# Half of the next head's rows ahead of a head's attention product, in an eight-head graph attention kernel on one core

## The reference

```python
h = (x @ W).reshape(n, H, C)
alpha_s = jnp.einsum('nhc,hc->nh', h, a_s)
alpha_d = jnp.einsum('nhc,hc->nh', h, a_d)
e = jax.nn.leaky_relu(alpha_s[src] + alpha_d[dst], NEG_SLOPE)
m = jax.ops.segment_max(e, dst, num_segments=n)
e = jnp.exp(e - m[dst])
alpha = e / (segment_sum(e, dst)[dst] + EPS)
out = segment_sum(h[src] * alpha[:, :, None], dst)
...
h = gat_layer(x, W1, a_src1, a_dst1, b1, edge_index, concat=True)
h = jax.nn.elu(h)
out = gat_layer(h, W2, a_src2, a_dst2, b2, edge_index, concat=True)
x = _layernorm(x + out, axis=-1)
```

## Time and profile before

| | before |
|---|---|
| median of 3 runs | 640.83 us (640.81 to 641.07) |
| the profiled execution | 641.08 us |
| its span in the profile | 639.3 us |
| TensorE busy | 632.1 us (99%) |
| VectorE, ScalarE, GpSimd busy | 518.9, 337.8, 204.4 us |

### The profile page before, as it was taken

One profiled execution on the slowest core, in us unless ns is written; L12 is line 12 of the kernel. 1 busy time (PEld: TensorE's weight loads), 2 busy tenths in 40 slices (PEclk: granted clock), 3 DMA queues, 4 the chain that ended last, 5 costly groups with the idle time before them and its releaser, 6 DMA issues.

```text
span 639.3 us, 9306 instructions
## 1 busy us (share of the span) xinstructions
PE 632.1 (99%) x3426; PEld 542.7 (85%) x3426; DVE 518.9 (81%) x928; ACT 337.8 (53%) x570; POOL 204.4 (32%) x122
## 2 busy tenths in 40 slices
PE   9999999999999999999999999999999999999996
PEld 6766568989888889988898889988998899887885
DVE  8999997889989987475855685567898589889876
ACT  7899992546524754353545454463545444534382
POOL 1000000140743630357124822374136604551230
PEclk9999999999999999999999999999999999999999
DMA  8422402115154420234113330316025401800002
GB/s 313 166 75 75 154 20 99 50 54 194 51 148 140 158 74 1 60 91 148 50 51 91 97 110 25 95 45 183 26 90 159 123 26 51 293 28 1 1 2 99
DMA packets 22173, 59.36 MB, mean 93 GB/s; under 512 B 2544, under 2 KB 2800, under 8 KB 22128
## 3 DMA queue, kind: packets, MB, share of 16 engines
q1 hardware_dynamic: 21984, 58.69, 28.6%
q10 hardware_dynamic: 144, 0.07, 0.0%
HBM read 54.03 MB, written 4.72 MB: 92 GB/s over the span
## 4 chain that ended last, share of the span: by engine, by line
PE 82%; DVE 16%; issue 1%; DMA 0%; ACT 0%; DVEq 0%
PE O L1238 30%; PE R L1136 8%; PE R L1133 8%; PE R L1139 8%; PE R L1205 6%; PE R L1211 6%; PE R L1208 6%; DVE ohd L679 4%; DVE ohs L683 2%; PE O L1150 2%; DVE junk L717 2%; DVE junk L736 2%; PE R L1155 1%; DVE W1l L705 1%; PE O L1205 1%
## 5 line engine op out<-in xcount | busy, mean ns | idle before, releaser
L1066 POOL TENSOR_TENSOR W2l<-Wr,W2h 128x768 fp32r<-128x768 f32 x48 | 93.3, 1953 | 207.8 <-ACT W2h L411 207.8
L1070 POOL TENSOR_TENSOR Pl<-L,Ph 128x512 fp32r<-128x512 f32 x34 | 54.0, 1599 | 166.7 <-ACT Ph L460 166.4
L1133 PE MATMUL R<-W1h,xTh 128*128 128x384 f32 x312 | 105.8, 339 | 0.0
L1139 PE MATMUL R<-W1h,xTl 128*128 128x384 f32 x312 | 104.9, 336 | 0.0
L1136 PE MATMUL R<-W1l,xTh 128*128 128x384 f32 x312 | 104.8, 336 | 0.0
L717 DVE CUSTOM_DVE_ANT_0 junk<-h,abc 128x768 bf16<-128x768 f32 x64 | 62.6, 978 | 41.8 <-ACT h L423 37.4
L1238 PE MATMUL O<-W2h,gh 128*128 128x256 f32 (+1 forms) x384 | 78.6, 339 | 0.0
L1238 PE MATMUL O<-W2h,gl 128*128 128x256 f32 (+1 forms) x384 | 77.4, 336 | 0.0
L1238 PE MATMUL O<-W2l,gh 128*128 128x256 f32 (+1 forms) x384 | 77.3, 335 | 0.0
L423 ACT COPY h<-R 128x384 f32<-128x384 f32 x62 | 29.5, 477 | 73.0 <-PE R L1139 70.9
L1060 POOL TENSOR_TENSOR W1l<-Wr,W1h 128x768 fp32r<-128x768 f32 x30 | 55.4, 1868 | 37.5 <-ACT W1h L400 37.5
(11 more groups left out here) (186 smaller groups left out, 1171.5 us busy)
## 6 DMA issues: line engine op xcount, KB each, us to landing
Wr<-in_W SPq DMA_DIRECT2D x101, 384.0 KB, 3.3
abc<-in_as SPq DMA_DIRECT2D x9, 384.0 KB, 4.0
abc<-in_ad SPq DMA_DIRECT2D x9, 384.0 KB, 5.9
h_rows<-h SPq DMA_DIRECT2D x8, 384.0 KB, 2.4
hl<-h_rows SPq DMA_DIRECT2D x8, 384.0 KB, 5.9
xin<-in_xT SPq DMA_DIRECT2D x6, 256.0 KB, 6.1
xr<-in_x SPq DMA_DIRECT2D x1, 1536.0 KB, 7.5
out<-res SPq DMA_DIRECT2D x4, 384.0 KB, 2.3
```

Source lines behind the costliest of these rows:

```text
L1066: e.tensor_tensor(W2l[:, m % N2, :], Wr[:, n, :], W2h[:, m % N2, :].bitcast(f32), ALU.subtract).then_inc(s_w2l, 1)
L1070: e.tensor_tensor(Pl[:, t, d0:d1], L[:, t, d0:d1], Ph[:, t, d0:d1].bitcast(f32), ALU.subtract).then_inc(s_Pl, 1)
L1133: e.matmul(bank[:, 0:HALF], xTh[:, f, xs], hi[:, ws], start=f == 0, stop=False)
L1139: m = e.matmul(bank[:, 0:HALF], xTl[:, f, xs], hi[:, ws], start=False, stop=f == FT - 1)
```

## The change

On TensorE, from head 3 on, the first four halves of B of head h+1 (tiles 0 and 1) are multiplied between the fifth and the sixth step of C(h-1), before den and A of head h; the other four stand at the start of head h+1 as before. `targets` moves from behind the second step of C to behind the third (heads 3 to 6). RING follows. On the other engines the work is written in another order around this, and the six pairs of products with the last layer's vectors are placed anew: pairs 0, 1 before the scores of head 5, pairs 3, 4 before those of head 6, pair 2 in head 6 and pair 5 in head 7 behind a tile's row sums. No instruction of arithmetic is added or taken away.

```diff
-    V_OF = {H - 3: range(0, 3), H - 2: range(3, 6)}
+    V_ROWS, V_SCORES = {H - 2: (2,), H - 1: (5,)}, {H - 3: (0, 1), H - 2: (3, 4)}
...
-    for h in range(EARLY, H):
-        RING += [("B", h, n) for n in range(8)]
-        RING += [("as", h, 0), ("r2", h, 0), ("r1", h, 0), ("den", h, 0)] + [("A", h, c) for c in range(FT)]
+    for h in range(EARLY, H + 1):
+        RING += [("B", h, n) for n in range(4) if h < H]
+        RING += [("den", h - 1, 0)] + [("A", h - 1, c) for c in range(FT)]
+        if h < H:
+            RING += [("B", h, n) for n in range(4, 8)] + [("as", h, 0), ("r2", h, 0), ("r1", h, 0)]
...
# scalar_program, head h
+                    if h + 1 < H:
+                        high_w1(h + 1, 0)
+                        high_w1(h + 1, 1)
                     high_w2(h - 1, 4)
+                    scores(h, h, 0, NT, ring_bank("r2", h, 0), (gl_value(h - 1, FT - 1), (s_g, FT * h)), 3 * h + 2,
+                           lambda u, h=h: high_w1(h + 1, 1 + u) if h + 1 < H and 1 <= u <= 4 else None)
+                    if h + 1 < H:
+                        evict_B(h + 1, 0, 0)
+                    high_sums(h)
                     high_w2(h - 1, 5)
+                    if h + 1 < H:
+                        evict_B(h + 1, 0, 1)
+                        high_w2(h, 0)
+                        evict_B(h + 1, 1, 0)
+                        high_w2(h, 1)
+                        evict_B(h + 1, 1, 1)
+                        high_w2(h, 2)
...
# vector_program, head h
-                    for t in range(NT):
+                    for t in (2, 3):
...
                     maxima(h, 0, NT, ring_bank("as", h, 0))
+                    if h + 3 == H:
+                        wait_abc(H)
+                    for i, k in enumerate(V_SCORES.get(h, ())):
+                        products_W2(k, 0 if i else 8 * h + 8)
                     scores(h, h, 0, NT, ring_bank("r1", h, 0), 3 * h + 3)
                     sums_P(h)
...
+                if 2 <= h < H - 1:
+                    wait_abc(h + 1)
+                    for t in range(2):
+                        e.wait_ge(s_h32, 8 * (h + 1) + 2 * t + 2)
+                        sums_h(h + 1, t, h32[:, t, :], abc[:, abc_slot(h + 1)[0], :, :])
                 if h:
                     reciprocals(h)
...
# gpsimd_program, head h
                 if h >= EARLY:
-                    for k in range(FT):
-                        low_w2(h - 1, k)
+                    if h + 1 < H:
+                        low_w1(h + 1, 0)
+                        low_w1(h + 1, 1)
+                    low_w2(h - 1, 4)
+                    if h + 1 < H:
+                        for k in range(2, FT):
+                            low_w1(h + 1, k)
                 for t in range(NT):
                     low_P(h, t, 0, N)
-                if EARLY <= h < H - 1:
-                    for k in range(FT):
-                        low_w1(h + 1, k)
+                if h >= 2:
+                    low_w2(h - 1, 5)
+                    if h + 1 < H:
+                        for k in range(4):
+                            low_w2(h, k)
...
# tensor_program, head h
                 if h >= EARLY:
-                    for n in range(8):
+                    for n in range(4, 8):
                         half_B(h, n // 2, n % 2, take("B", h, n))
                 for c in range(2 if h == 1 else 0, FT):
+                    if c == FT - 1 and 2 <= h < H - 1:
+                        for n in range(4):
+                            half_B(h + 1, n // 2, n % 2, take("B", h + 1, n))
                     stage_C(h - 1, c, between=(lambda h=h: denominators(h)) if c == FT - 1 else None,
                             at=1 if h == H - 1 else 2)
-                    if c == (0 if h == 2 else 1) and h > 1:
+                    if c == (0 if h == 2 else 1 if h == H - 1 else 2) and h > 1:
                         targets(h, 0, NT, (None, None), 2 * h + 2)
```

More of the change, by code:

```diff
@@ L37, in gat_resnorm_kernel @@
     for h in range(EARLY, H):
-        LOADS += [("w2", h - 1, k) for k in range(FT)]
-        LOADS += [("w1", h + 1, k) for k in range(FT) if h + 1 < H]
-        LOADS += [("v", H - 1, k) for k in V_OF.get(h, ())]
+        LOADS += [("w2", h - 1, k) for k in range(4)] + [("v", H - 1, k) for k in V_ROWS.get(h, ())]
+        LOADS += [("w2", h - 1, 4)] + [("w1", h + 1, k) for k in range(2) if h + 1 < H]
+        LOADS += [("v", H - 1, k) for k in V_SCORES.get(h, ())]
+        LOADS += [("w1", h + 1, k) for k in range(2, FT) if h + 1 < H] + [("w2", h - 1, 5)]
     LOADS += [("w2", H - 1, k) for k in range(FT)]
@@ L51, in gat_resnorm_kernel @@
     RING += [("as", 2, 0), ("den", 1, 0)] + [("A", 1, c) for c in range(FT)]
-    RING += [("r2", 2, 0), ("r1", 2, 0), ("den", 2, 0)] + [("A", 2, c) for c in range(FT)]
-    for h in range(EARLY, H):
-        RING += [("B", h, n) for n in range(8)]
-        RING += [("as", h, 0), ("r2", h, 0), ("r1", h, 0), ("den", h, 0)] + [("A", h, c) for c in range(FT)]
+    RING += [("r2", 2, 0), ("r1", 2, 0)]
+    for h in range(EARLY, H + 1):
[3 more added lines that the diff above has]
+            RING += [("B", h, n) for n in range(4, 8)] + [("as", h, 0), ("r2", h, 0), ("r1", h, 0)]
     RING += [("al", H, 0), ("at", H, 0), ("as", H, 0), ("r2", H, 0), ("r1", H, 0), ("tail", 0, 0)]
@@ L335, in sync_program @@
             for h in range(EARLY, H):
+                if h + 2 < H:
+                    load_abc(h + 1)
+                for k in range(4):
+                    load_raw("w2", h - 1, k)
+                for k in V_ROWS.get(h, ()):
+                    load_raw("v", H - 1, k)
+                load_raw("w2", h - 1, 4)
                 if h + 1 < H:
[L337 to L339 removed]
+                    load_raw("w1", h + 1, 0)
+                    load_raw("w1", h + 1, 1)
+                if h + 3 == H:
+                    load_abc(H)
                 if h + 2 == H:
                     load_abc(H - 1)
+                for k in V_SCORES.get(h, ()):
+                    load_raw("v", H - 1, k)
                 if h + 1 < H:
[L343 removed]
+                    for k in range(2, FT):
                         load_raw("w1", h + 1, k)
[L345 to L346 removed]
+                load_raw("w2", h - 1, 5)
             for k in range(4):
@@ L565, in scalar_program @@
                     high_sums(2)
+                    evict_B(3, 0, 0)
                     high_h(2, 2)
                     high_h(2, 3)
+                    high_w2(1, 5)
+                    evict_B(3, 0, 1)
+                    high_w2(2, 0)
+                    evict_B(3, 1, 0)
+                    high_w2(2, 1)
+                    evict_B(3, 1, 1)
+                    high_w2(2, 2)
                 if 0 < h < EARLY:
@@ L603, in scalar_program @@
                 for c in range(FT):
+                    if c == FT - 1 and 2 <= h < H - 1:
+                        high_h(h + 1, 0)
                     exp_y(h, c)
+                    if c == FT - 1 and 2 <= h < H - 1:
+                        high_h(h + 1, 1)
                     if c:
                         high_g(h, c - 1)
+                    if c == FT - 1 and 2 <= h < H - 1:
+                        evict_B(h + 1, 2, 0)
                     if h == 0 and c < 2:
@@ L614, in scalar_program @@
                         high_w1(3, c - 2)
-                    if EARLY <= h < H - 1 and c < 2:
-                        high_w1(h + 1, 4 + c)
+                    if 2 <= h < H - 1 and c == 1:
+                        high_w2(h, 3)
                     if h == H - 1 and c == 0:
@@ L714, in sums_h @@
                         e.wait_ge(s_asd, n)
-                    if not i and h - 1 in V_OF and t in range(1, 4):
-                        e.wait_ge(s_v, 2 * V_OF[h - 1][t - 1] + 2)
+                    if not i and t == 0 and h - 1 in V_SCORES:
+                        e.wait_ge(s_v, 2 * V_SCORES[h - 1][-1] + 2)
+                    if not i and t == 3 and h in V_ROWS:
+                        e.wait_ge(s_v, 2 * V_ROWS[h][-1] + 2)
                     e.tensor_tensor_reduce(
@@ L730, in products_W2 @@
                 for i in range(2):
-                    if i:
-                        e.wait_ge(s_v, 2 * k + 1)
+                    if i or not ready:
+                        e.wait_ge(s_v, 2 * k + i)
                     else:
@@ L945, in vector_program @@
                         low_h(h, t)
[L946 to L949, removed]
+                        if t == 2:
+                            for k in V_ROWS.get(h, ()):
+                                products_W2(k, 8 * h + 6)
                     maxima(h, 0, NT, ring_bank("as", h, 0))
+                    if h + 3 == H:
+                        wait_abc(H)
+                    for i, k in enumerate(V_SCORES.get(h, ())):
+                        products_W2(k, 0 if i else 8 * h + 8)
                     scores(h, h, 0, NT, ring_bank("r1", h, 0), 3 * h + 3)
@@ L968, in vector_program @@
                         part_sums(3)
-                    if c > 1:
```

(3 more changed lines are left out.)

41 lines of the change are left out of this document (16 added, 25 removed).

## The result

The changed kernel takes 655.25 us in the median against 640.86 us: 1.0224 times as long, 95% interval 1.019 to 1.0258, so it is slower. The forecast had the direction and the mechanism of the gaps, but 655.25 lies above its 650.0 and just outside its range (646.0 to 654.7). The profiled execution took 653.75 us, its span grew from 639.3 to 651.9, by 12.6 us.

What follows compares the result with a forecast made beforehand. TensorE, 99% busy, was taken to bound the kernel. Four waits of 2.4 us less 0.43 for r12 gave +9.2 on the profiled 641.08, so 650.3, as a median 650.0 us; range 646.0 to 654.7.

Steps and rivals of the forecast that it cites:

- The slack and the gap: Heads 3 to 6: reciprocal must start by T+4.0 but starts at T+6.4, so TensorE waits 2.4 us per head (1.4 to 3.4).
- T: The moment when TensorE has issued the last early half of B in a head; forecast at Z+20.9, Z being the first score's start.
- a round: One VectorE row sum taking turns with one GpSimd W2l subtraction: 2.51 us in place of 1.0.
- They run one after the other: VectorE's row sums and GpSimd's W2l subtractions block each other; whoever waited goes first, so each sum stands behind a W2l.
- Rivals 1 and 2: 1: one round instead of four, 641.4 us, chance 0.05; 2: no collision, not slower, 640.4 us, chance 0.04.
- rival 3: W1l loses over 1.3 us more, so the first early half waits and scores are late: 655 to 658 us, chance 0.06.
- r12, -0.43: Head 7: TensorE's wait for VectorE's late r12 goes, since one pair of products, not three, stands among its row sums: -0.43 us.
- TensorE's own work keeps its length; an early half costs 3.12 us where it now stands, as before: TensorE: instruction counts are the same on every engine, so the moved matmuls of B were booked at no cost.
- No run here shows it for a gap of this size: Clock behind TensorE's stalls: a fall to 1.2 GHz after a 2.4 us gap was unshown, so given chance 0.03.
- rival 4: The clock falls to 1.2 GHz for a column behind each stall, 2.76 us each: +11, 661 us, chance 0.03.

Runs made afterwards that it cites:

- e1: Changed kernel, with four W2l subtractions on POOL in heads 3 to 6 waiting for the head's reciprocal; 642.09 us, 1.0018 of the kernel before.
- e3: Changed kernel, with two of VectorE's four row sums in heads 3 to 6 moved behind the first scaling; 642.13 us, 1.0018 of the kernel before.
- e2: Changed kernel, with only two of the four W2l subtractions (rows 2 and 3) waiting for the reciprocal; 646.01 us, 1.0079 of the kernel before.
- e4: Kernel before, with only the products with the last layer's vectors spread over heads 5 to 7; 641.24 us, ratio 1.0003.
- e8: As e4, with the two products ahead of the scores of heads 5 and 6 moved behind g; 640.72 us, 0.9999 of the kernel before.
- e7: As e1, with three added 128x512 matmuls ahead of each of the five early halves; 644.30 us, 1.0054 of the kernel before.
- e5: Changed kernel again, no edit, one execution for its profile; 657.1 us.
- e6: As e1, but the wait on POOL applies from head 4 on, leaving head 3 as changed; 645.38 us, 1.0067 of the kernel before.
- e9: Changed kernel, with the reciprocal of heads 3 to 6 done twice to lengthen each gap; 673.83 us, 1.0515 of the kernel before.

## Why the prediction was right or wrong, step by step

The steps on the wait were right; the step that failed is that TensorE's work outside the wait keeps its length, with the pace, the restart behind a gap and the clock all booked at nothing.

- **The slack and the gap: right.** With T = 304.60, the second column was due at T+7.38 (forecast T+7.39), the first W2l started at T-4.0 (T-3.8), the first sum 0.53 us behind it (0.3), and the reciprocal at T+6.26 (T+6.4). Gap 2.27 to 2.29 us against 2.4, four of them, none in heads 2 and 7. e1 and e3 show that it needs both, POOL's queue and the sums ahead of the reciprocal; e2 shows the price of a round, 1.52 us over a sum alone.
- **"They run one after the other": right.** By the Trainium skill, "SBUF — State Buffer", Who interferes with whom, one of such a pair blocks the other whole; the 2.23 and 0.96 us of e1 agree. Rivals 1 and 2 are out, and so is rival 3: TensorE shows no gap ahead of an early half.
- **r12, -0.43: right as a mechanism** (e4, e8), but by itself below what runs can tell.
- **"TensorE's own work keeps its length; an early half costs 3.12 us where it now stands, as before": wrong.** Counts were the same, the pace was not. An early half behind C takes 3.18, and eight blocks cost 1.9 us. e1 and e3, without a gap, keep six slow blocks (1.4 us) and are 1.1 us slower than the kernel before. Why the pace changes stays open. The first matmul behind each gap, 0.11 us longer, was not in the sum either.
- **"No run here shows it for a gap of this size", and so 0.03 for the clock: wrong.** It fell behind some of the gaps, not all, and for eight matmuls, not a column of twelve: 1.6 or 4.7 us, where I had 0 or, as rival 4, 11. The only gap in the earlier trace rows with the clock at 1.00 was of 0.43 us, so it spoke neither for nor against; the range should have held up to four falls.
- The sum: forecast +9.2 in the span; the gaps, r12 and the first stages gave 9.1 - 0.4 + 0.1 = 8.8; the restart 0.4, the pace 1.9 and the clock 1.6 make the 12.7, and two more falls the upper level. The lower level, 653.7, lies inside the forecast range by luck, since the upper bound was set for a longer wait than came; the upper level lies outside, and the median, a time between the levels that no run has, is 0.55 us outside.

No version is faster than the kernel before by what runs can tell: e8 equals it, and e1 and e3 mend the change to 1.0018.

## What to carry to other kernels

Before work is moved on VectorE ahead of an operation that releases a bank, list what GpSimd does in that stretch: here a row sum with two SBUF inputs cost 0.96 us alone and 2.2 to 2.5 beside a queue of GpSimd subtractions. A cure can stand on either side, one wait on GpSimd or two sums behind the release. Where the matmul engine is 99% busy, as here, only its waits can be won by a new order of the work (0.43 us here), and a gap of some us should be priced with a fall of the clock, as a range.

## What was not expected of the hardware

- A block of 128x384 matmuls has two paces, 173.3 and 176.6 to 176.8 ns. All 35 early blocks directly behind C, in seven profiles, have the slower one, and all five behind three added 128x512 matmuls the faster (e7). Of the 55 blocks behind A, in all eleven profiles, 13 have the slower one, one of them in e4, where no matmul was moved and TensorE only paused for 0.09 us some 18 us earlier.
- The granted clock stayed at 1.0 behind four gaps of 0.75 us (e2), fell to 0.5 (1.2 GHz) behind five of nine gaps of 2.27 to 2.29 us (one of four, three of four in e5, one of one in e6) and behind four of four of 5.7 us (e9). What chooses among equal gaps stays open.
